# Attention block on one core: scores and weighted values in plain float32 on 32x64 tiles of TensorE, weights transposed by VectorE

## The reference, cut to what matters

```python
x: (64, 128, 512)   attn_bias: (16, 128, 128)   H, DH = 16, 64
xn = layernorm(x, g_in)
q = (xn @ Wq) -> 16 heads of 64, times DH ** -0.5
k, v = xn @ Wkv                       # one key and one value head for all 16
k, v = concat(null_kv, k), concat(null_kv, v)
sim = q @ k.T + concat(null_bias, attn_bias)
sim = where(causal or masked key, -max, sim)
out = softmax(sim) @ v                # 16 heads, 128 rows, 129 keys
out = layernorm(out @ Wo, g_out)
return x + out
```

## Time and profile before

| | us |
|---|---|
| median of 3 runs | 1217.46 (1216.24 to 1217.88) |
| the profiled execution's own time | 1217.43 |
| its span, first to last instruction | 1215.6 |
| PE busy | 1178.6 |
| DVE busy | 980.4 |
| ACT busy | 983.9 |
| POOL busy | 828.8 |

### The profile page before, as it was taken

One profiled execution on the slowest core, in us unless ns is written; L12 is line 12 of the kernel. 1 busy time (PEld: TensorE's weight loads), 2 busy tenths in 40 slices (PEclk: granted clock), 3 DMA queues, 4 the chain that ended last, 5 costly groups with the idle time before them and its releaser, 6 DMA issues.

```text
span 1215.6 us, 34031 instructions
## 1 busy us (share of the span) xinstructions
PE 1178.6 (97%) x8320; PEld 1086.5 (89%) x8320; DVE 980.4 (81%) x4249; ACT 983.9 (81%) x3434; POOL 828.8 (68%) x1520
## 2 busy tenths in 40 slices
PE   4799999999999999999999999999999999999996
PEld 4699998999999999999999999999999999999994
DVE  6778888888788788888888788788888888788873
ACT  4878887888888888887888888888887888888873
POOL 2647767667677667767667677676766677677676
PEclk9899999999999999999999999999999999999999
DMA  6101111111111111111111111111111111111011
GB/s 201 54 20 55 40 53 36 36 55 54 37 54 35 37 54 55 36 54 36 36 55 54 37 52 38 37 54 55 36 53 37 36 55 54 37 50 40 19 36 53
DMA packets 39282, 58.47 MB, mean 48 GB/s; under 512 B 9792, under 2 KB 13376, under 8 KB 39104
## 3 DMA queue, kind: packets, MB, share of 16 engines
q1 hardware_dynamic: 36992, 54.81, 14.1%
q10 hardware_dynamic: 2112, 2.10, 0.5%
HBM read 40.11 MB, written 16.78 MB: 47 GB/s over the span
## 4 chain that ended last, share of the span: by engine, by line
PE 89%; POOL 3%; issue 2%; DVE 2%; ACT 1%; POOLq 0%; DVEq 0%; ACTq 0%
PE ps_proj L456 32%; PE ps_o L449 28%; PE ps_s L411 10%; PE ps_wt L421 7%; PE ps_pv L435 7%; PE ps_pv L438 3%; PE ps_proj L473 2%; POOL bias_b L863 1%; POOL w_nrm L872 1%; PE ps_proj L483 1%; POOL y_nrm L908 0%; DVE q_sb L623 0%; DVE s_low L531 0%; ACT exp_bot L744 0%; POOL y_out L912 0%
## 5 line engine op out<-in xcount | busy, mean ns | idle before, releaser
L872 POOL TENSOR_TENSOR w_nrm<-exp_bot,w_inv 128x256 f32<-128x256 f32 x256 | 157.5, 615 | 319.2 <-DVE w_inv L552 313.4
L863 POOL TENSOR_TENSOR bias_b<-bias_c,mask_add 128x256 f32<-128x256 f32 (+1 forms) x512 | 295.6, 598 | 0.1
L456 PE MATMUL ps_proj<-xt_hi,wq_hi 128*128 128x256 f32 x1024 | 290.0, 283 | 5.2 <-DVE q_sb L623 3.8
L456 PE MATMUL ps_proj<-xt_lo,wq_hi 128*128 128x256 f32 x1024 | 289.5, 283 | 0.0
L456 PE MATMUL ps_proj<-xt_hi,wq_lo 128*128 128x256 f32 x1024 | 289.3, 282 | 0.0
L796 ACT CAST q_sb<-ps_proj 64x256 fp32r<-64x256 f32 x512 | 187.7, 367 | 113.3 <-PE ps_proj L456 97.4
L623 DVE TENSOR_TENSOR q_sb<-ps_proj,q_sb 64x256 fp32r<-64x256 f32 x512 | 216.3, 422 | 25.8 <-ACT q_sb L796 14.3
L449 PE MATMUL ps_o<-wo_hi,o_hi 128*128 128x512 f32 x512 | 223.5, 437 | 0.2 <-DVE o_lo L565 0.2
L744 ACT ACTIVATE exp_bot<-logit_bot,neg_max 128x129 f32<-128x129 f32 x512 | 202.2, 401 | 10.9 <-DVE neg_max L543 6.6
L449 PE MATMUL ps_o<-wo_lo,o_hi 128*128 128x512 f32 x512 | 202.8, 396 | 0.0
L449 PE MATMUL ps_o<-wo_hi,o_lo 128*128 128x512 f32 x512 | 202.8, 396 | 0.0
(11 more groups left out here) (92 smaller groups left out, 2569.0 us busy)
## 6 DMA issues: line engine op xcount, KB each, us to landing
x_in<-in_x_dram SPq DMA_DIRECT2D x32, 512.0 KB, 3.5
x_res<-in_x_dram SPq DMA_DIRECT2D x64, 256.0 KB, 2.7
out_dram<-y_out SPq DMA_DIRECT2D x64, 256.0 KB, 2.0
w_raw<-in_L_cond_Wq_dram ACTq DMA_DIRECT2D x4, 512.0 KB, 8.1
w_raw<-in_L_cond_Wo_dram SPq DMA_DIRECT2D x4, 512.0 KB, 6.4
mask_u<-in_mask_BxS_bk_dram SPq DMA_DIRECT2D x32, 32.0 KB, 3.3
bias_c<-in_fside_16xSxS_dram SPq DMA_DIRECT2D x4, 128.0 KB, 6.9
y_nrm<-in_L_cond_Wkv_dram SPq DMA_DIRECT2D x1, 256.0 KB, 6.6
```

The lines of the kernel that those rows point to most:

```text
L456: mm = pe.matmul(ps[:, 0:TOK], w[:, k, cols], xt[:, k], start=(j == 0), stop=(j == len(todo) - 1))
L863: ins = nc.gpsimd.tensor_tensor(out_, bias, key_mask, ALU.add)
L872: ins = nc.gpsimd.tensor_tensor(out_, w_exp[:, s, :, 0:keys_], w_inv[:, s, 2 * i:2 * i + 2].unsqueeze(2).to_broadcast([P, 2, keys_]), ALU. ...
```

## The change

The projections (`project`, `project_out`) stay as they are. The attention between them is rebuilt:

- **Scores** are plain float32 products. The 64 numbers of a head are cut in two runs of 32 partitions (`half`), and each matmul uses 32 partitions and 64 columns of the array. `score` issues, for two steps at once, 32 matmuls with 128 or 64 moving columns. `ps_s` then holds complete scores, so `scores_low` and `s_low` are gone, and `logits` reads score and bias directly.
- **Weights** are transposed in 32x32 blocks by VectorE (`transposed`, one instruction of 128x384 a step, SBUF to SBUF). `weights_t`, `ps_wt`, `wt_hi` and `wt_lo` are gone.
- **Values** are used in 32-row runs (`v32`) that are made by eight copying transfers (`spread_v`) and one block transpose (`spread_v_of`) for each group. The product of weights and values is plain float32 in 32x64 tiles, 20 matmuls of 128 columns for each two steps. Their partition runs are the two that the scores beside them do not use.
- **Visits**: scores and values are issued together in `visit`, once for two steps, in two halves with a wait on TensorE's own results between them.
- **Queries** are copied whole by VectorE (one copy of 128x256 for two heads) with no rounding and no remainder.
- The lags are now in a table `PLAN`; the output projection is issued in two pieces of 12 matmuls a batch. The two projection buffers alternate by group.

```diff
+PLAN = {"pv_a": 6, "pv_b": 8, "heads": 8, "out_a": 9, "out_b": 11, "stats": 12, "scale": 13, "norm": 14, "add": 15}
...
+LAG_SUM, LAG_NORM, LAG_T = 1, 1, 2
...
-            def scores(n, g, t):
...
-                for late in (1, 0):
-                    wait(pe, s_read, 2 * n - late)
-                    for e in range(2):
-                        mm = pe.matmul(ps_s[:, 2 * (1 - late) + e].rearrange("p a n -> p (a n)"),
-                                       q_sb[:, slot, c, e, 2 * b + late].rearrange("p u n -> p (u n)"),
-                                       keys[:, slot, b].rearrange("p a n -> p (a n)"), start=True, stop=True)
+            def score(p, t, half, r):
+                slot, b = t // CG, t // CB % GB
+                if r > 2:
+                    return
+                for e in range(2):
+                    rows = slice(BLK * (2 * e + half), BLK * (2 * e + half + 1))
+                    scored = ps_s[e][:, 0:2 * WIDE].rearrange("p (s n) -> p s n", s=2)
+                    for u in range(2):
+                        for s, late in (((0, 1),), ((1, 1),), ((0, 0), (1, 0)))[r]:
+                            from_ = N * b + HALF * late
+                            mm = pe.matmul(scored[HALF * u:HALF * (u + 1), s, 0:N] if late else
+                                           scored[HALF * u:HALF * (u + 1), s, N:WIDE],
+                                           q_sb[rows, slot, t % CB + s, u, from_:from_ + HALF],
+                                           keys[rows, slot, b, 0:N if late else HALF],
+                                           start=(half == 0 and r == 0), stop=(half == 1 and r == 2 and s == 1))
...
-            def weights_t(n, t):
...
+            def values(back, part, half, r):
...
+                for u in range(2):
+                    rows = slice(BLK * (2 * u + qh), BLK * (2 * u + qh + 1))
+                    for e in range(2):
+                        block = N // BLK * e + j if late else 2 * (N // BLK) + HALF // BLK * e + j
+                        at = HALF * late + BLK * qh
+                        mm = pe.matmul(ps_pv[u][DH * e:DH * (e + 1), :, at:at + BLK], v32[rows, slot, b, j],
+                                       wt[rows, b, block],
+                                       start=(qh == 1 and part == 0 and r == 0),
+                                       stop=(qh == 0 and part == 1 and r == len(items) - 1))
+            def visit(p, t, first, last):
...
+                if scoring:
+                    wait(pe, s_read, 4 * m)
...
+                for half in range(2):
+                    if half == 1:
+                        if scoring:
+                            pe.wait_ge(s_half, 4 * m + 4)
+                        if parts:
+                            batch, back, part = parts[-1]
+                            pe.wait_ge(pv_half, 8 * batch + 4 * part + 4)
...
+                    for r in range(max(3 * scoring, len(todo))):
+                        if scoring:
+                            score(p, t, half, r)
+                        if r < len(todo):
+                            values(*todo[r][:2], half, todo[r][2])
...
             def logits(n, t):
...
+                            out_[:, e, 0:keys_], ps_s[e][:, from_:from_ + keys_], bias[:, e], -1.0, 0.0,
+                            ALU.add, ALU.min, neg_max[:, s, 2 * i + e:2 * i + e + 1])
...
-                nc.vector.tensor_tensor(wt_lo[:, s], ps_wt[:], wt_hi[:, s].bitcast(F32),
-                                        ALU.subtract).then_inc(wt_lo_made, 1)
+                nc.vector.transpose(wt[:, par, :, c], w_nrm[:, s]).then_inc(wt_made, 1)
...
+                elif kind == "q":
+                    wait(dve, proj_done, USES * f + use + 1)
+                    nc.vector.tensor_copy(q_sb[:, slot, i // 2, i % 2], ps[:, 0:TOK]).then_inc(q_made, 1)
```

More of the change, by code:

```diff
@@ L278, in bot_top @@
             return row[:, 0:BOT].rearrange("p (e n) -> p e n", e=2), row[:, BOT:].rearrange("p (e n) -> p e n", e=2)
[L280 to L293, removed]
         def steps(last):
@@ L300, in live, with due @@
             return not (first and t < lag) and t - lag < CP
[L302 to L307, removed]
+        def due(what, p, t, first, last):
+            for back in range(-3, 4):
+                plan = PLAN_63 if last and back == 3 else PLAN_62 if last and back == 2 else PLAN
+                if 4 * back + plan[what] == t and not (first and back < 0):
+                    yield 2 * GB * p + back, back
         def front_parts(p, t, first, last):
-            if (first and t < 0) or t >= CP:
+            if t >= CP:
                 return
-            for kind, i, ahead in FRONT_FIRST[t] if first and t < CG else FRONT[t % CG]:
+            table = FRONT_FIRST if first and t < CG else FRONT
+            for kind, i, ahead in table.get(t % CG, ()):
                 if last and t // CG + ahead == 2:
@@ L390, in _, with body @@
-            with sp.Fori(0, PAIRS - 2) as p:
-                body(p, True, False)
-            body(PAIRS - 2, False, False)
-            body(PAIRS - 1, False, True)
-            for b in range(GB):
-                sp.wait_ge(stored[b], 16 * GROUPS)
+                if i == 1:
+                    spread_v(0)
+            for i in range(GB):
+                load_res(0, i)
+            load_x_and_mask(1, 0)
+            def body(p, first, loads, last):
+                spread_v(2 * p + 1)
+                if not first:
+                    store(p, -3, True)
+                    store(p, -2, True)
+                if not last:
+                    load_x_and_mask(p + 1, 1)
+                    spread_v(2 * p + 2)
+                if not first:
+                    store(p, -1, True)
+                if loads:
+                    load_x_and_mask(p + 2, 0)
+                store(p, 0, True)
+                if last:
+                    store(p, 1, True)
+                    store(p, 2, False)
+                    store(p, 3, False)
@@ L446, in project_out @@
+            def project_out(batch, back, part):
+                b = back % GB
+                wait(pe, o_lo_made, 2 * batch + 2)
+                if part == 0:
                     wait(pe, y_nrm_made, batch - 1)
-                todo = [(o, w, i) for i in range(2) for o, w in ((o_hi, wo_hi), (o_hi, wo_lo), (o_lo, wo_hi))]
+                todo = [(o, w, i) for i in range(OT // 2 * part, OT // 2 * (part + 1))
+                        for o, w in ((o_hi, wo_hi), (o_hi, wo_lo), (o_lo, wo_hi))]
@@ L703, in body @@
                         inverse(n - LAG_SUM, t - LAG_SUM)
-                    if done := out_batch(p, t, STEP_OUT_STATS + 1, first, last):
-                        out_mean_var(*done)
-                    if not last and t % CG == STEP_STATS + 1:
-                        x_mean_var_of(2 * p + t // CG + 2)
+                    for batch, back in due("heads", p, t, first, last):
+                        for u in range(2):
+                            heads_lo(batch, u)
+                    for part in front_parts(p, t, first, last):
+                        front(*part)
@@ L708, in body @@
+                    if live(t, LAG_T, first, last):
+                        transposed(n - LAG_T, 2 * GB * p + (t - LAG_T) // CB, (t - LAG_T) % CP)
                     if t < CP:
-                        logits(n, t)
+                        for done in due("stats", p, t, first, last):
+                            out_mean_var(*done)
                     if first and t in first_extras:
                         first_extras[t]()
-                    if live(t, LAG_HEADS, first, last) and (t - LAG_HEADS) % 2:
-                        heads_lo(pair(p, t - LAG_HEADS), t - LAG_HEADS)
```

447 lines of the change are left out of this document (194 added, 253 removed).

## The result

| | before | after |
|---|---|---|
| median, us | 1217.67 | 1285.79 (4 runs, 1280.11 to 1290.3) |
| span of the profiled execution | 1215.6 | 1285.6 |

A forecast was written before the change was run, and what follows sets the result against it. TensorE was taken as the bound: 879.4 us kept + 273 for visits + 35 for new waits - 28 for old bias and weight waits - 2.6 for the tail = 1157 us; the 8-in-10 range was 1080 to 1450.

The forecast's parts named there:

- What stays (the projections, the input transposes) is untouched: On TensorE, dropping five kinds of matmuls saves 338 us and leaves the rest unchanged, 879.4 us.
- in-line rivals: TensorE's tiles overlap only with neighbours (1650 us, chance 0.12) or not at all (2300 us, chance 0.03).
- The visit: TensorE's scores and values for two steps: 2.1 us each, 130 of them 273 us; break-even at 2.6 us.
- joints: Drained start, wait between halves and following projection in a visit: 0.83 us, bounds nothing and twice that.
- column price: Plain float32 product on TensorE: twice the transpose, 0.214 us per 128 columns; lower end 0.107.
- The two waits of 0.55 us: TensorE waits for VectorE in a group's first and fifth steps: 1.1 us a group, 35 us over 32 groups.
- VectorE and ScalarE as cover: VectorE falls to about 22.3 us a group, ScalarE loses 9.7 of 30.7; both stay hidden behind TensorE.
- Small instructions are the price: Rival: a floor per load-and-matmul pair sets the visit's 52 pairs; 1330 us at 0.05, 1500 at 0.075; chance 0.18.
- Only neighbours overlap: Rival: the next tile cannot start before the previous product's second pass; visit 5.9 us, time 1650 us; chance 0.12.
- VectorE's order takes over: Rival: VectorE's work before the fifth step's visit delays it if the block transpose costs 1.1 us; 1190 us; chance 0.06.
- The tail: At the end, the last two output projection pieces come together, closing a gap of 2.6 us.

The follow-up runs named there:

- a_pe_straight: The changed kernel with TensorE's sixteen passes written out instead of looped, other engines as they were: 1199.29 us, ratio to before 0.9859.
- a_all_straight: The changed kernel with the passes of TensorE, VectorE, ScalarE and GpSimd all written out: 1187.6 us, ratio to before 0.9766.
- a_tile_by_tile: The changed kernel with TensorE's passes written out and each tile's matmuls issued in a row instead of in turns: 2151.32 us, ratio to before 1.7635.
- a_scores_then_values: The changed kernel with TensorE's passes written out and, in each half-visit, all score matmuls issued before the values' matmuls: 1250.32 us, ratio to before 1.027.
- b_dve_straight: The kernel before with VectorE's passes written out, TensorE's loop kept: 1208.05 us, ratio to before 0.9932.

## Why the prediction was wrong

**The step that failed** is "What stays (the projections, the input transposes) is untouched: 1217.4 - 338 = 879.4 us", and with it the whole form of the sum: it priced what is executed and not what has to be brought. I counted 104 loads and matmuls a visit for the rival on small instructions, but never added them up over a pass. 2320 against 1040 was to be had from the page and the diff, and the trace of before had VectorE waiting 35.4 us for "issue", about once a pass. In its place the runs show 86.5 us that TensorE spends on being loaded anew and on the low clock behind it: 1285.79 with the loop, 1199.29 without, and the projections that were to stay untouched take 3.8 to 5.3 us instead of 3.04 for 24 of them behind each of the 13 jumps (chain of after). None of the rivals was this one either. That 1286 lay inside the range is luck: the in-line rivals had stretched it, and the 0.36 for "slower" stood on causes that did not come.

**The account.** Forecast 1157. TensorE's reloads, with the half clock behind them: + 86.5 (a_pe_straight). VectorE's: + 11.7 (a_all_straight, which frees ScalarE and GpSimd too). A group away from them: 35.1 against 36.5 - 338 / 32 + 4 x 2.1 + (35 - 28) / 32 = 34.56 in the forecast, 32 x 0.54 = + 17. The ending: the last input transposes of before and of after end at

```profile
L473 PE MATMUL ps_proj<-ident,xn x256: 272/273/445, 10.0 to 1140.2; 128*128 128x128 f32 x128
```

```profile
L482 PE MATMUL ps_proj<-ident,xn x256: 270/273/444, 11.8 to 1196.1; 128*128 128x128 f32 x128
```

75.4 and 89.5 us ahead of the end of the span: + 14 where 2.6 were to be gained, so + 17. TensorE waits there three times for VectorE's heads, 7.1 us in all, which the forecast did not count, and the granted clock of this stretch is 0.92 (0.98 before). Its pieces behind such waits are

```profile
1243.10 4.61 PE ps_o L457 x12
...
1269.67 7.44 PE ps_o L457 x24
```

at up to 0.38 us a matmul, where the earlier trace rows have 2.90 / 12 = 0.24. In sum 1289, 3 above what was measured. One term is missing that goes the other way: the transposes of the second and third group start 40.7 us apart in before and 32.0 in after, and nothing in the forecast priced that start. The rest is left open.

**Step by step.**
- *The visit*, 2.1 us forecast, 2.27 measured: right, under the break-even of 2.6. With 1.28 for the streams that leaves 0.99 for the joints, where 0.83 was taken. The column price of twice the transpose was right: passes of 0.107 to 0.11, two of them a product. The Trainium skill (FP8 and Floating Point Precision, section Matmul Precision) gives true float32 four passes. The trace has two records a product, each at half the rate of float32r (0.107 us for 128 columns against 0.115 for 256): in time, that is four.
- *The two waits of 0.55 us*: not there. Of 17 us for each in the whole run, the matmuls of the input transposes show 0.3, the later projections none, and the weight loads of the transposes 7.4, which overlap other work. The 11.1 us in a_pe_straight are another thing, VectorE's reload. The weight loads' group (busy, mean ns, idle before):

```profile
L482 PEld LDWEIGHTS ps_proj<-ident,xn 128*128 128x128 f32 x256 | 28.2, 143 | 21.3 <-issue 12.3 <-DVE q_sb L605 7.4
```

- *VectorE and ScalarE as cover*: right. VectorE is busy 704.1 / 32 = 22.0 us a group (22.3 forecast), ScalarE 20.5 (21).
- *Small instructions are the price*: wrong in its mechanism. In its own terms (2.27 - 0.83) / 52 = 0.028 us a product, under the 0.034 from which it decides. Their number did cost, by the length of the loop's body.
- *Only neighbours overlap*: wrong for this order, and real for another: a_tile_by_tile is that kernel. The Trainium skill's rule of starts in program order (TensorE: Matmul & The Clock Gate, Part 3, "What overlaps and what doesn't") doesn't hold between tiles here: in a_scores_then_values score passes start behind values that follow them in the program.
- *VectorE's order takes over*: not seen; the transpose is at 0.564 and not 1.1.
- *The tail*: wrong, as above.

The forecast's idea was sound: between the versions without reloads of TensorE and VectorE, b_dve_straight at 1208.05 and a_all_straight at 1187.6, the change is worth 20 us, a third of the 60 that were forecast.

## What to carry to other kernels

Before replacing few large instructions by many small ones inside a hardware loop, add up the loop body of each engine, weight loads included: here 1040 matmuls and loads of TensorE stayed, 2320 were brought again at every jump, and that cost 6.7 us each time. The sign in a trace is a wait for "issue" once a pass, with many more instruction packets than the program's length needs; writing the loop out cured it here. And with tiles of the array side by side, let them take turns in the program: the same work cost 1199 us in turns and 2151 tile by tile.

## What was not expected of the hardware

- A jump back costs TensorE more than the load: 3.65 us idle, and then the 1.2 GHz level, 5.17 us for 24 projections instead of 3.05.
- A program of 147 packets written out runs at 1199 us: straight code of 2.41 MB is brought while it runs, with no "issue" wait over 1.1 us on TensorE.
- Eight 32x64 tiles start their first passes within 0.07 us when they take turns.
- Tile after tile, TensorE had a record open for 1190 of 1200 us, and still the granted clock was 0.76: "busy" in the page does not keep the 2.4 GHz level. The projections behind a visit began at half speed (0.58 us for the first at 614.67, against 0.39 at 602.21 in after).
